# Attention stage of a macaron layer: the maxima are turned and negated earlier in their step, the reciprocals of the sums later in the round

## What is computed

```python
x = x + 0.5 * ffn(layernorm(x))
x = x + attention(layernorm(x))
x = x + 0.5 * ffn(layernorm(x))
```

## Time and profile before

| | us |
|---|---|
| median of 3 runs | 1507.14 (1503.88 to 1508.54) |
| the profiled execution's own time | 1502.69 |
| its span in the trace | 1500.7 |
| PE busy | 1421.7 (95%) |
| DVE busy | 955.8 (64%) |
| ACT busy | 661.6 (44%) |
| POOL busy | 584.5 (39%) |

### The profile page before, as it was taken

How to read it: one execution, slowest core, us unless ns; L and a number is a source line. 1 busy time by engine, 2 the same in 40 slices (tenths; PEclk the granted TensorE clock), 3 DMA queues, 4 the chain that set the end, 5 groups by cost and what they waited for, 6 DMA issues and landing times. The chain is left out here.

```text
span 1500.7 us, 28646 instructions
## 1 busy us (share of the span) xinstructions
PE 1421.7 (95%) x8712; PEld 1158.5 (77%) x8712; DVE 955.8 (64%) x2269; ACT 661.6 (44%) x1347; POOL 584.5 (39%) x832
## 2 busy tenths in 40 slices
PE   5999999999999968999999999889999899999998
PEld 2688878888878866677677776558888788888887
DVE  5679865655645657777676766535786455565566
ACT  4524444344333434665665665553322243343332
POOL 6538810233333013464465454321288333333100
PEclk9999999999999988999999999879999999999999
DMA  9988998534395946345554555445564634356941
GB/s 347 347 314 294 324 357 320 168 123 128 121 335 170 306 136 150 87 119 150 137 136 120 132 130 134 134 143 202 179 242 148 230 105 145 105 199 207 311 128 57
DMA packets 176534, 285.80 MB, mean 190 GB/s; under 512 B 20738, under 2 KB 125698, under 8 KB 176146
## 3 DMA queue, kind: packets, MB, share of 16 engines
q1 hardware_dynamic: 134642, 206.31, 43.8%
q0 software_dynamic: 19104, 56.64, 10.4%
q10 hardware_dynamic: 22656, 21.11, 4.8%
HBM read 144.20 MB, written 109.84 MB: 169 GB/s over the span
## 5 line engine op out<-in xcount | busy, mean ns | idle before, releaser
L1709 PE MATMUL f_bank<-f_xparts,f_sw 128*128 128x512 f32 x1536 | 375.5, 394 | 4.7 <-DVEq L1639 3.3
L1709 PEld LDWEIGHTS f_bank<-f_xparts,f_sw 128*128 128x128 f32 x1536 | 282.6, 190 | 60.0 <-DVEq L1639 4.3
L1160 POOL DMA_INDIRECT outputs_by_choice<-f_yr,f_home x160 | 153.4, 959 | 360.1 <-DVE f_yr L1663 294.5
L2323 ACT ACTIVATE at_pT<-at_ps 128x512 f32<-128x512 f32 (+1 forms) x352 | 189.7, 560 | 66.6 <-PE at_ps L2589 59.5
L2251 POOL TENSOR_SCALAR_AFFINE_SELECT at_pT<-at_pT 128x128 f32<-128x128 f32 (+2 forms) x352 | 122.1, 355 | 211.1 <-ACT at_pT L2323 209.1
L1118 POOL DMA_INDIRECT rows_by_slot<-f_xq,slot x128 | 145.9, 1140 | 123.6 <-DVEq L1390 85.3
L1545 DVE TENSOR_TENSOR f_hid<-f_sil,f_bank 128x512 f32<-128x512 f32 x128 | 87.7, 686 | 131.5 <-PE f_bank L1709 97.5
L1652 DVE TENSOR_TENSOR f_sil<-f_sil,f_bank 128x256 f32<-128x256 f32 x160 | 67.4, 421 | 162.6 <-ACT f_sil L1294 156.2
L1274 ACT CAST f_hparts<-f_hid 128x512 fp32r<-128x512 f32 x128 | 79.4, 620 | 202.1 <-DVE f_hid L1545 188.6
L2589 PE MATMUL at_ps<-fa_qT,fa_kT 98*128 98x256 f32 (+3 forms) x512 | 156.6, 359 | 9.7 <-DMA fa_qT<-at_mT 7.5
L2565 PE MATMUL at_ps<-fa_kT,fa_qT 96*128 96x512 f32 (+2 forms) x384 | 149.9, 407 | 3.3 <-DVE at_mx L2439 2.9
(11 more groups left out here) (264 smaller groups left out, 2522.6 us busy)
## 6 DMA issues: line engine op xcount, KB each, us to landing
f_ring<-weights_in_parts SPq DMA_DIRECT2D x32, 768.0 KB
weights_in_parts<-fa_whi SPq DMA_DIRECT2D x30, 768.0 KB, 9.2
f_rawx<-rows_by_slot ACTq DMA_DIRECT2D x152, 128.0 KB
at_whi<-weights_in_parts SPq DMA_DIRECT2D x16, 768.0 KB
fa_ew<-in_L_ffn_routed_w_dram SPq DMA_DIRECT2D x42, 256.0 KB, 5.4
rows_by_slot<-zero POOLq DMA_DIRECT2D x10, 1024.0 KB, 22.2
f_xq<-xn_rows POOLq DMA_DIRECT2D x32, 256.0 KB
fa_ew<-outputs_by_choice SPq DMA_DIRECT2D x8, 1024.0 KB, 8.6
```

Source lines behind the costliest of these rows:

```text
L1160: nc.gpsimd.indirect_dma_start(dram.yk, bass.IndirectOffsetOnAxis(ap=home[:, i:i + 1], axis=0), yr[:, i % 4, :], None).then_inc(y_st[i % 4 ...
L1709: ins = pe.matmul(ps[j % 2][:, :], sw12[:, wp, k, w, j * P:(j + 1) * P], xparts[:, u, xp, k, :], start=(i == 0), stop=(i == 3 * KD - 1))
L2323: s_.activation(pT[:, i % SLOTS, 0:w], ps2[i % RING2][:, 0:w], ACT.Exp).then_inc(ex_done, 1)
```

## The change

The reciprocals of a half move from step 1 to step 3, their sending from step 2 to step 3, and the fetch from step 4 to step 5. On the DVE `shift` goes ahead of `maxima` of the same step. On the PE `turn_max` goes ahead of `score2` of the same step. Nothing is computed otherwise, and no operation is added or removed.

```diff
-    AT_TURN, AT_SEND, AT_FETCH, AT_OUT = 1, 2, 4, (2, 6)
+    AT_TURN, AT_SEND, AT_FETCH, AT_OUT = 3, 3, 5, (2, 6)
...
                 for s in range(UN):
+                    if max_of(i, s) is not None:
+                        shift(i)
                     if 0 <= i + 1 < TG:
                         maxima(i + 1, s)
-                    if max_of(i, s) is not None:
-                        shift(i)
                     if s == AT_TURN and half_of(i) is not None:
                         turn_over(*half_of(i))
...
                     if 0 <= i + 1 < TG:
                         score1(i + 1, s)
+                    if max_of(i, s) is not None:
+                        turn_max(i)
                     u = i * UN + s - LAG
                     if 0 <= u < TG * UN:
                         score2(u // UN, u % UN)
-                    if max_of(i, s) is not None:
-                        turn_max(i)
```

## The result

The changed kernel takes 1549.36 us in the median of 6 runs (1548.36 to 1553.66), the kernel before 1507.96 (1503.88 to 1512.09, 6 runs): a ratio of 1.0276, 95% interval 1.0254 to 1.0297. The change costs 41 us. The profiled execution took 1549.71 us, with a span of 1547.9.

What follows compares the result with a forecast made beforehand. The attention's steady part was taken as PE-bound, with some 13 us of PE idle. The terms -14 + 23.2 + 13.8 + 12 = +35 on the profiled 1502.69 us gave 1538 us, range 1512 to 1562.

Steps and rivals of the forecast that it cites:

- waits of before that go: Attention stage: PE waits at `project` and for the copy of the maxima should go, 14 us of 15.3 saved.
- stops at `score1`, remainder 0: Even rounds after remainder 3: late fetch delays `scale`, the maxima and step 4's `score1`; 3.3 us, 7 times, 23.2 us.
- stops at `project_out`, remainder 2: Even rounds after remainder 1: `project_out` waits for the late `scale`; 2.3 us, 6 times, 13.8 us lost.
- lower clock: PE clock falls behind the seven longer stops, 1.7 us each, 12 us; nothing for the six shorter ones.
- rounds 29 and 31 have no `lay_out` and lose nothing: Last attention rounds: no copies of `lay_out` ahead of the fetch there, so no loss was counted.
- The landing time: Fetch behind `lay_out`: 4.6 us from issue to landing, against 4.1 us for a lone fetch.
- the fetch is hidden anyway: Rival at `scale`: the fetch lands before `scale` is reached, so the kernel gets faster, 1489 us; chance 0.08.
- the fetch lands fast: Rival: the fetch lands as fast as a copy of `lay_out`, about 2.7 us, giving 1501 us; chance 0.06.
- the clock holds: Rival: the PE's clock does not fall at the stops, +23 us, 1526 us; chance 0.25.
- the reciprocal was not what held `shift`: Rival on the DVE: the 14 us gain does not come, the loss stays, 1552 us; chance 0.05.
- more is lost: Rival: landing of 6.0 us, later maxima, or the clock falling at all thirteen stops; 1550 to 1570 us; chance 0.16.
- That the maxima of step 2 begin later: DVE, behind the earlier `shift`: priced at 0, with an upper end of 0.6 us a round, 19 us.

Runs made afterwards that it cites:

- filled kernel: The changed kernel with useless matmuls put where the PE would stop, ahead of `score1` and `project_out`'s step: 1528.45 us, ratio 1.0149 to the kernel before.
- the gaining version: The changed kernel with the fetch back in step 4, ahead of `lay_out`'s nine copies: 1486.07 us, ratio 0.9868 to the kernel before.
- the fourth kernel: The kernel before with reciprocals and their sending moved to step 3, fetch left in step 4, order within steps unchanged: 1494.31 us, ratio 0.9914.

## Why the prediction was right, and where it was off

The direction, the place and the mechanism were right, and the time lies in the range; the forecast was +31 us against the median (+35 against the profiled execution, which is the sum below), and +41 was measured. The terms of the sum:

| term | forecast | measured | by what |
|---|---|---|---|
| waits of before that go | -14 | about -20 (-27 to -12) | kernel with the fetch in step 4, 0.9868 |
| stops at `score1`, remainder 0 | +23.2 | +23.5 | waits after |
| stops at `project_out`, remainder 2 | +13.8 | +18.5 | waits after |
| lower clock | +12 | +19 (11 to 27) | filled kernel, 0.0127 |
| sum | +35 | +41 | ratio 1.0276 |

That the four measured terms add up to 41 to the microsecond is luck, since two of them are known to some 8 us. The forecast is near in part by luck too: the costs were reckoned 12 us too small and the gain 6 us, and the two partly cancel.

*The waits that go.* The prediction took 14 of 15.3 us. It added 7.5 us, which the PE waited, to 7.8 us, which is a row of its weight loads (PEld). The PE's own row there, before, is shorter:

```profile
PE at_psX L2614 <- DVE at_mT L2448: 4.5, 7, 1.2
```

So the PE waited 12.0 us at these two places, and 4.2 are left with the fetch in step 4. The windows, which hold all of its idle, went from 12.6 of 355 us before to 2.9 of 345, about 10 us. The clock gave the rest. The steady stage ran at 0.98 before and at 1.00 in the gaining version; 0.02 of 355 us is 7 us, a gain that the prediction did not look for. 10 and 7 make 17 of about 20. The 0.98 comes of three stretches at half clock, at 748.4, 902.0 and 946.3 us. Only the last lies by stops of the PE (1.47 and 1.12 us); the other two begin 0.9 and 0.8 us behind 16 small matmuls (L2688, 16 columns each), which all versions have. Why these stretches are missing with the fetch in step 4 is open.

*The stops at `score1`.* The price of 3.3 us was made for round 16 and taken seven times. The rounds differ, from 2.7 to 3.8 us, and the mean met it, but not by its parts. The fetch landed 0.45 us sooner than the 4.6 us reckoned. From the first copy of `lay_out` to the fetch, SP needed 5.8 us in rounds 7, 11, 23 and 27, as reckoned, and 6.5 to 6.6 in rounds 3, 15 and 19, where it was held at one copy; behind those three stand the stops of 3.7 and 3.8 us.

*The stops at `project_out`.* Here the step "rounds 29 and 31 have no `lay_out` and lose nothing" failed. Round 29 has three loads of the next stage's weights and rows in step 4, and they went ahead of the fetch too. SP's timeline after, round 29, with the fetch behind them, and `scale` of round 30:

```profile
995.16 1.09 SPq L2214 DMA_DIRECT2D f_raw<-in_L_ffn_shared_w_dram  x2
996.29 0.60 SPq L2217 DMA_DIRECT2D at_raw<-xn_turned  x1
996.99 0.66 SPq L2173 DMA_DIRECT2D at_rec<-one_over_sums  x1
```

```profile
1004.56 0.69 DVE L2475 TENSOR_TENSOR at_attnT<-at_av,at_rec 128x512 f32<-128x512 f32 x1 [1.24 <-DMA at_rec<-one_over_sums]
```

The fetch took 7.6 us and round 30's `project_out` stopped for 1.5 us. The other 3.2 us are nearly all in round 6, which stopped for 5.3 us where 2.3 was reckoned; the five rounds behind it stopped for 1.2 to 3.5 us and average 2.3. The price was made for round 17's length and taken for all; round 5 has no second turn and no routing yet (they belong to the sequence two before), so it lasts 10.45 us from one turn of the maxima to the next, where rounds 9 to 25 last 12.6 to 13.5. The fetch of the first such half is needed that much sooner.

*The landing time.* 4.6 us was reckoned. In the thirteen rounds it was 3.9 to 4.6 us, 4.15 in the median, by the last arrival on the fetch's semaphore; the lone fetch was the right row, and the copies under way ahead of it did not slow it. By the rule on ring order that the prediction takes from the Trainium skill, DMA: Bandwidth & Descriptors, Queues, rings and completion order, a landing above the lone 4.1 us was to be expected; behind the nine copies the trace does not show it. That the place behind nine copies hurts comes from SP's 5.7 us of issuing.

*The clock.* This is the term that was mis-sized. The prediction let the clock fall behind the seven longer stops alone. The trace has thirteen stretches at half clock from 620 to 985 us, ten of 3.4 us and three of 6.8, and none there in the filled kernel. Twelve of them begin in or just behind a stop of the PE, and stops of 2.2 us, as in round 18, have one as well as those of 3.7 us. The stretch at 888 us began ahead of round 22's stop, 0.9 us behind the 16 small matmuls, like the two of before; what set it off is open. The thirteen hold 54 us, which at half speed is 27 us at most; 19 were measured. By the warning of the Trainium skill, TensorE: Matmul & The Clock Gate, Why this matters for your kernels, against idle gaps between bursts of matmuls, the forecast was right to count the clock at all; the trace agrees, by 19 us.

The rivals: *the fetch is hidden anyway* and *the fetch lands fast* fall by the row of `scale`, 15 waits; *the clock holds* falls by the thirteen stretches and the filled kernel; *the reciprocal was not what held `shift`* falls by the fourth kernel, 0.9914. Of *more is lost*, one condition came true, the clock falling at nearly all thirteen stops, and the time stands just below its 1550; the landing of 6.0 us did not come. That the maxima of step 2 begin later costs nothing that shows: the kernel with the swaps alone is faster than before.

## What to carry to other kernels

When a step is moved in a schedule written by hand, write down each queue's list before and after, the DMA queue's too: the constant that moved the fetch by one step of about 1 us moved it by nine copies, 5 us, because another step's work stood between. A part of a change can lose more than the whole, and a bundle of three edits with two good ones is worth taking apart: the fetch in its old place turns 2.8% slower into 1.3% faster. Short stops of the PE are dearer than their length where they bring the clock down; here 42 us of stops took about another 19.

## What was not expected of the hardware

Useless matmuls made the kernel faster by about 19 us, as the granted clock stayed at 1.00 with them in the place of stops of 1 to 5 us. And the time of the fetch to its landing depends more on what is issued behind it than on what is under way ahead of it: 3.9 to 4.6 us with `lay_out` ahead (median 4.15 of 13, after), 4.7 to 7.5 with `lay_out` behind (median 5.7 of 13, before), and about 5.0 with three copies behind. Behind the loads of the next stage it is longer: 7.6 us in round 29 and 6.1 in round 31, one case each.
